# Five reorderings in a four-layer attention and expert kernel: masks and a table made earlier, VectorE's step order, a norm without transposes, a sum by additions, extra matmuls around a norm

## What is computed

```python
x = x + _L1_xattn_ref(_layernorm(x, axis=-1), ctx_2048, ctx_2048)
x = x + _L1_ffn_ref(_layernorm(x, axis=-1), L1_ffn_gate_weight, L1_ffn_gate_up_proj, L1_ffn_down_proj, L1_ffn_similarity)
x = x + _L2_xattn_ref(_layernorm(x, axis=-1), ctx_2048, ...)
x = x + _L2_ffn_ref(_layernorm(x, axis=-1), ...)
x = x + _L3_xattn_ref(_layernorm(x, axis=-1), ctx_2048, ctx_2048, mask, ...)
```

```python
sim = sim.at[jnp.arange(E), jnp.arange(E)].set(1.0)
sim_cand = sim[sec[:, :, None], prim[:, None, :]]
new_sec = jnp.where(best_sim < THRESHOLD, sec, best_primary)
combine = jnp.sum(jax.nn.one_hot(rerouted_indices, E) * routing_weights[..., None], axis=1)
```

## Time and profile before

| | |
|---|---|
| median of 3 runs | 1818.53 us (1818.27 to 1819.35) |
| profiled execution | 1817.0 us |
| its span | 1815.3 us |
| mean granted clock of PE | 0.890 |
| PE busy | 1519.1 us (84%) |
| DVE busy | 1083.3 us (60%) |
| ACT busy | 805.5 us (44%) |
| POOL busy | 801.4 us (44%) |
| layer two: norm, attention | 458.4 to 466.5, 466.8 to 571.8 us |
| layer two: feed-forward part | 573.7 to 853.9 us |
| layer three: attention after its preparation | 897 to 1297.5 us |
| layer four: norm, attention | 1480.3 to 1488.4, 1488.7 to 1578 us |

### The profile page before, as it was taken

The page is one execution under the profiler, slowest core; times in us unless marked ns, Lnnn a source line. Parts: engine busy times, 40 slices in busy tenths (PEclk is TensorE's granted clock), DMA queues, the critical chain, the costliest instruction groups (busy, mean ns, idle before and its releaser), DMA issues. The chain is left out here.

```text
span 1815.3 us, 25122 instructions
## 1 busy us (share of the span) xinstructions
PE 1519.1 (84%) x8563; PEld 971.4 (54%) x8600; DVE 1083.3 (60%) x2317; ACT 805.5 (44%) x1879; POOL 801.4 (44%) x975
## 2 busy tenths in 40 slices
PE   7566669999797799998899999999799989836772
PEld 5222235556465356556367777776455565525661
DVE  7999972222665644354778888888722255572336
ACT  3988873111333211111788888888521111412221
POOL 3366641000200289792277787777310000027772
PEclk9666659999698899999999999999899988958896
DMA  2599981110503111310600000000111100056656
GB/s 79 86 182 176 174 150 55 35 44 18 186 2 124 64 55 59 125 50 19 209 1 13 13 13 13 13 13 1 44 30 42 37 25 1 25 219 233 233 172 243
DMA packets 177808, 148.52 MB, mean 82 GB/s; under 512 B 142305, under 2 KB 155233, under 8 KB 173970
## 3 DMA queue, kind: packets, MB, share of 16 engines
q1 hardware_dynamic: 167618, 119.08, 24.3%
q0 software_dynamic: 7696, 26.22, 4.1%
q10 hardware_dynamic: 2368, 1.61, 0.3%
HBM read 89.62 MB, written 23.70 MB: 62 GB/s over the span
## 5 line engine op out<-in xcount | busy, mean ns | idle before, releaser
L1983 POOL CAST l0m_pi<-l0m_pf 128x1024 bf16<-128x1024 int16 x128 | 133.2, 1040 | 88.2 <-ACT l0m_pf L2050 86.4
L421 PE MATMUL l1e_gu<-x_normT,l1e_w 128*128 128x512 f32 x384 | 171.5, 601 | 0.0
L2050 ACT ACTIVATE l0m_pf<-l0m_s,l0m_bias,l0x_sq 128x1024 int16<-128x1024 f32 x128 | 153.9, 1204 | 20.9 <-DVE l0m_bias L2083 14.7
L2079 DVE TENSOR_REDUCE l0m_mx<-l0m_s 128x1 f32<-128x1024 f32 x128 | 155.6, 1216 | 4.4 <-PE l0m_s L1992 4.1
L1558 PE MATMUL l2x_pr<-l_w,l2x_xq 128*128 128x512 bf16 x539 | 133.5, 382 | 8.5 <-ACT credits L42 5.7
L1992 PE MATMUL l0m_s<-l0x_kT,l0x_qT 64*128 64x512 bf16 x256 | 68.0, 552 | 68.5 <-ACT l0m_pf L2050 66.9
L421 PE MATMUL l0e_gu<-x_normT,l0e_w 128*128 128x512 f32 x272 | 121.5, 601 | 0.0
L421 PEld LDWEIGHTS l1e_gu<-x_normT,l1e_w 128*128 128x128 f32 x384 | 74.2, 194 | 84.1 <-issue 83.0
L421 PE MATMUL l2e_gu<-x_normT,l2e_w 128*128 128x512 f32 x256 | 115.0, 604 | 0.0
L1688 DVE BATCH_NORM_STATS2 l2x_bn<-l2x_raw 128x6 f32<-128x128 f32 x384 | 83.3, 280 | 51.7 <-ACT l2x_raw L1627 51.5
L473 ACT ACTIVATE l1e_sil<-l1e_gu 128x512 f32<-128x512 f32 x48 | 28.6, 596 | 178.6 <-PE l1e_gu L421 178.6
(11 more groups left out here) (438 smaller groups left out, 3597.1 us busy)
## 6 DMA issues: line engine op xcount, KB each, us to landing
l3m_w<-in_l_moe SPq DMA_DIRECT2D x16, 1280.0 KB, 6.9
l1e_w<-in_l_ffn SPq DMA_DIRECT2D x24, 384.0 KB, 3.1
l_rows<-zero_row SPq DMA_DIRECT2D x8, 1024.0 KB, 10.9
l_w<-l_rows SPq DMA_DIRECT2D x8, 1024.0 KB, 11.3
l0e_w<-in_l_ffn SPq DMA_DIRECT2D x17, 384.0 KB, 3.1
l2e_w<-in_l_ffn SPq DMA_DIRECT2D x16, 384.0 KB, 3.0
ctx_tok<-l_route SPq DMA_DIRECT2D x8, 512.0 KB
l2q_wps<-in_l_wp SPq DMA_DIRECT2D x16, 256.0 KB, 3.5
```

The costliest lines, as they stand in the source:

```text
L421: last = nc.tensor.matmul(gu[half][:, m, :], w[:, c % SW, (2 * k + m) * P:(2 * k + m + 1) * P], pg.xnT[:, k, cols(n)], start=(k == 0), sto ...
L1983: nc.gpsimd.tensor_copy(pi[:, n % 8, :], pf[:, n % 4, :]).then_inc(s["rounded"], 1)
L2050: nc.scalar.activation(pf[:, n % 4, :], s_ps[n % 3][:], ACT.Exp, scale=sq[:, h, b:b + 1], bias=bias[:, n % 4:n % 4 + 1], accum_out=sm[:, b ...
L2079: nc.vector.tensor_reduce(mx[:, n % 4:n % 4 + 1], s_ps[n % 3][:], AX, ALU.max).then_inc(s["maxed"], 1)
```

## The change

It has five parts.

1. `norm` gets a switch `turns`, off for layer two's attention: PE's 16 transposes and their eight copies out are left out there.
2. Layer two's masks `quarter`, `own`, `other` are made by POOL at the end of its list in layer one's feed-forward part (`l1_masks`). In the attention POOL first waits for DVE's two small `qm` pieces before it zeroes `nm`, and for all four before it touches `vz`, of which it now zeroes only the columns that aren't copied. The four copies of context columns go from POOL to ACT, behind `cb`. DVE waits for the zeroed `nm` after `qm`.
3. Layer two's router gets its table as a whole 128 x 128 array by one DMA in the stage's preload; POOL only sets the diagonal. ACT does a dummy exponential at the start of its list. The final reduction over eight rows becomes three additions of halves.
4. In layer three's attention, the norm's multiplication and the reciprocal come first in DVE's list of each step.
5. `keep_busy` adds PE matmuls of the identity by itself (128 x 128, f32) into unused PSUM: eight at the end of layer three's feed-forward part, eight before the transposes of layer four's norm, and two between each pair of those.

```diff
+def l1_masks(pg, pool):
+    g, C, steps = pg.nc.gpsimd, 16, pg.sem("l1_mask_steps")
+    quarter, own, other = (pg.l1_masks[:, n, :] for n in range(3))
+    g.memset(quarter, 1.0 / 4.0).then_inc(steps, 1)
...
+    g.tensor_scalar(own, quarter, 4.0, None, ALU.mult).then_inc(steps, 1)
+    g.tensor_scalar(other, quarter, -4.0, 1.0, ALU.mult, ALU.add).then_inc(steps, 1)
...
+def keep_busy(pg, unread, n):
+    for _ in range(n):
+        pg.nc.tensor.matmul(unread, pg.ident[:], pg.ident[:], start=True, stop=True)
...
-            for i in range(PAIRS):
+            if warm:
+                keep_busy(pg, ps[0][0][:, 0:P], 8)
+            for i in range(PAIRS if turns else 0):
...
+                if warm and i + 1 < PAIRS:
+                    keep_busy(pg, ps[i + 1][0][:, 0:P], 2)
...
+            if name == "l2":
+                keep_busy(pg, gu[0][:, 0, 0:P], 8)
...
-        nc.gpsimd.memset(r.sim[:], 0.0).then_inc(r.const_steps, 1)
-        pool.wait_ge(r.const_in, 16 * S)
+        pool.wait_ge(pg.l1_sim_in, 16)
...
+        nc.scalar.activation(r.small[:, 3, 0:1], pg.ident[:, 0:1], ACT.Exp).then_inc(r.const_in, 1)
         exp_scalar(r, act)
...
-        v.tensor_reduce(r.cw[:], r.one.rearrange("p b k e -> p b e k"), AX, ALU.add).then_inc(r.route, 1)
+        for n in (4, 2):
+            ch.link(v.tensor_tensor(r.one[:, :, 0:n, :], r.one[:, :, 0:n, :], r.one[:, :, n:2 * n, :], ALU.add))
+        v.tensor_tensor(r.cw[:], r.one[:, :, 0, :], r.one[:, :, 1, :], ALU.add).then_inc(r.route, 1)
...
+            pool.wait_ge(qm_in, 2)
+            g.memset(nm[:], 0.0).then_inc(zeroed, 1)
+            pool.wait_ge(qm_in, 4)
             for par in range(2):
...
-                    g.tensor_copy(vz[:, par, k, :].rearrange("p (n c) -> p n c", c=32)[:, :, cols],
-                                  pg.ctxT[:, k, :].rearrange("p (n c) -> p n c", c=32)[:, :, cols]).then_inc(vz_in, 1)
+                    g.memset(vz[:, par, k, :].rearrange("p (n c) -> p n c", c=32)[:, :, rest], 0.0).then_inc(vz_in, 1)
...
+                    nc.scalar.activation(vz[:, par, k, :].rearrange("p (n c) -> p n c", c=32)[:, :, cols],
+                                         pg.ctxT[:, k, :].rearrange("p (n c) -> p n c", c=32)[:, :, cols], ACT.Copy).then_inc(vz_copied, 1)
...
                     for t in range(8):
+                        if job := norm_due(t, 4, pi, ai):
...
+                            nc.vector.tensor_tensor(raw[:, u], raw[:, u], rs[:, 1, u].unsqueeze(2).to_broadcast([P, U, DH]), ALU.mult)\
+                                .then_inc(s["normed"], 1)
+                        if job := due(t, 4, ai, zi, wi):
...
+                            nc.vector.reciprocal(rsm[:, a % 2], sm[:, a % 2]).then_inc(s["recip"], 1)
                         if wi is not None and wi[1] == 1 and t == 2:
...
-            "l0f": lambda: ffn("l0", 9, router_l0, 17, 3, [(8, 1), (0, 8)], [6, 11], None),
+            "l0f": lambda: ffn("l0", 9, router_l0, 17, 3, [(8, 1), (0, 8)], [6, 11], l1_masks),
```

More of the change, by code:

```diff
@@ L83, in l2_centre @@
     return beside
+def l1_masks(pg, pool):
+    g, C, steps = pg.nc.gpsimd, 16, pg.sem("l1_mask_steps")
+    quarter, own, other = (pg.l1_masks[:, n, :] for n in range(3))
+    g.memset(quarter, 1.0 / 4.0).then_inc(steps, 1)
+    pool.wait_ge(steps, 1)
+    for par in range(2):
+        for j in range(4):
+            rows = slice(32 * j, 32 * j + 32)
+            g.affine_select(out=quarter[rows, par:par + 1], in_=quarter[rows, par:par + 1],
+                            compare_op=(ALU.is_gt if par == 0 else ALU.is_ge), fill=0.0,
+                            base=(C if par == 0 else -C), pattern=[[0, 1]],
+                            channel_multiplier=(-1 if par == 0 else 1)).then_inc(steps, 1)
+    pool.wait_ge(steps, 9)
+    g.tensor_scalar(own, quarter, 4.0, None, ALU.mult).then_inc(steps, 1)
+    g.tensor_scalar(other, quarter, -4.0, 1.0, ALU.mult, ALU.add).then_inc(steps, 1)
+    pool.wait_ge(steps, 11)
 def l2_split(pg, pool):
@@ L199, in negative_mean, with norm @@
                                             op0=ALU.mult, op1=ALU.mult).then_inc(self.nb_in, 1)
-def norm(pg, name, src, preload=None, twice=False, moments=None):
+def norm(pg, name, src, preload=None, twice=False, moments=None, turns=True, warm=False):
     nc = pg.nc
@@ L601, in allocate @@
         r.oneT = pg.xn[:, 0:B // 2, :].rearrange("p b d -> p (b d)")
-        r.sim = sb("sim", [P, P])
+        r.sim = pg.l1_sim
         r.w8 = sb("w8", [P, B, K])
@@ L629, in pe_prog @@
             last.then_inc(r.pe_done, 1)
[L630 removed]
+        pe.wait_ge(r.const_steps, 1)
         for g in range(2):
@@ L798, in psum @@
             return st.enter_context(nc.psum_tensor(f"l1x_{m}", shape, dt))
-        quarter = sb("quarter", [P, 2])
-        own = sb("own", [P, 2])
-        other = sb("other", [P, 2])
+        quarter, own, other = (pg.l1_masks[:, n, :] for n in range(3))
         qm = sb("qm", [P, 2, B, D])
@@ L908, in value @@
                 if q == 0:
-                    pe.wait_ge(vz_in, 2 + 2 + 2 * KD)
+                    pe.wait_ge(vz_in, 2 * (2 + KD))
+                    pe.wait_ge(vz_copied, 2 * KD)
                 for nh in range(KD):
@@ L933, in _ @@
         def _(act):
-            act.wait_ge(masks, 2)
             for half in split:
@@ L938, in _ @@
                                          bias=other[:, par:par + 1]).then_inc(cb_in, 1)
+            for par in range(2):
+                cols = slice(C * par, C * par + C)
+                for k in range(KD):
+                    nc.scalar.activation(vz[:, par, k, :].rearrange("p (n c) -> p n c", c=32)[:, :, cols],
+                                         pg.ctxT[:, k, :].rearrange("p (n c) -> p n c", c=32)[:, :, cols], ACT.Copy).then_inc(vz_copied, 1)
             for q in range(Q):
@@ L951, in _ @@
             v = nc.vector
-            dve.wait_ge(const, 10)
-            v.tensor_scalar(own[:], quarter[:], 4.0, None, ALU.mult).then_inc(masks, 1)
-            v.tensor_scalar(other[:], quarter[:], -4.0, 1.0, ALU.mult, ALU.add).then_inc(masks, 1)
             for half in split:
@@ L2435, in preload @@
                     sp.dma_start(pg.router_w[:], router_w).then_inc(pg.router_w_in, 16)
+                    if name == "l1":
+                        sp.dma_start(pg.l1_sim[:], dram["l1_sim"]).then_inc(pg.l1_sim_in, 16)
                     for c in range(slots):
@@ L2452, in attention @@
                 pre = preload_of(pg, early) if preload_of else None
-                norm(pg, f"{name}n", pg.x, pre.load if pre else None, name == "l2x")
+                norm(pg, f"{name}n", pg.x, pre.load if pre else None, name == "l2x", turns=(name != "l1x"), warm=(name == "l3x"))
                 pg.moments = Moments(pg, f"{name[:2]}n", nc.alloc_semaphore)
@@ L2510, in layout @@
     a["l1_router"] = halves(v["L1_ffn_gate_weight"].T)
-    a["l1_sim"] = v["L1_ffn_similarity"]
+    a["l1_sim"] = np.zeros((128, 128), np.float32)
+    for j in range(4):
+        a["l1_sim"][32 * j:32 * j + 32, 32 * j:32 * j + 32] = v["L1_ffn_similarity"]
     w = v["L1_ffn_gate_up_proj"]
```

45 lines of the change are left out of this document (13 added, 32 removed).

## The result

The changed kernel takes 1804.01 us (median of 4 runs, 1800.33 to 1807.2) against 1818.94 (1818.27 to 1820.73): a ratio of 0.9915, 95% interval 0.9901 to 0.993. 1803.1 was forecast, within 1798 to 1810.

What follows compares the result with a forecast made beforehand. No engine was taken to bound the whole program, so each part was priced in its place: -7.65 - 2.46 - 6.3 + 0 + 1.0 = -15.4 from the profiled 1817.0 gives 1801.6, plus 1.5 for the runs' median 1803.1, range 1798 to 1810.

Steps and rivals of the forecast that it cites:

- Layer two's start, -7.65: Layer two's attention: without transposes and late masks, the first maximum comes at 468.2 against 475.85, 7.65 us earlier.
- the cover: Layer two's attention: ACT, with its four moved copies, is ready 0.4 us before the first exponential is due.
- Router, -2.46: Layer two's router: 1.17 us less from the earlier table and 1.29 less from three additions replacing the reduction.
- Layer three, -6.3: Layer three's attention: 14 items each 0.40 us shorter, -5.6, and -0.7 in its last 25 us.
- the tail: Last 25 us of layer three's attention, bound by DVE: an earlier reciprocal gives 0.2 us in three to four steps, -0.7.
- The floor by ACT's copy of the one buffer: Layer three's transposes cannot start before ACT has read their one PSUM buffer, so 0.40 us per item is gained, not 0.82.
- The rival in which the wait only changes its name: Layer three: multiplication and POOL's L1520 collide, the 0.40 per item is lost again; layer gains 1, total 1808.4; chance 0.15.
- The slower rival: Layer three: later `bn_stats` delays POOL and PE's turn of the probabilities, each item 1.1 us longer; total 1824.8; chance 0.04.
- Layer four's norm, 0: Extra identity matmuls cost 1.0 us at layer three's end and save 0.8 in layer four's norm: net 0 (+0.2).
- Clock, +1.0: Allowance of 1.0 us for clock rises that come later after shifted starts, with ends of -1 and +4.

Runs made afterwards that it cites:

- a3_router: The kernel before with only layer two's router changed (table by one DMA, dummy exponential, three additions): ratio 0.9985 to the kernel before.
- second profile of the change: The changed kernel run and profiled once more with no edit: 1804.99 us.
- a1_order: The kernel before with only the norm's multiplication and the reciprocal put first in DVE's steps of layer three's attention: ratio 0.9964 to the kernel before.
- b1_norm_first: The kernel before with only the norm's multiplication moved ahead in layer three's attention, the reciprocal left in place: ratio 0.997 to the kernel before.
- c4_no_between: The changed kernel without the pairs of identity matmuls between layer four's norm transposes, the groups of eight kept: 1805.35 us against 1804.99.
- a2_l1x: The kernel before with only layer two's norm transposes left out, its masks made early and its context copies on ACT: ratio 0.9952 to the kernel before.
- a4_warm: The kernel before with only the identity matmuls at layer three's end and in layer four's norm: ratio 0.9987 to the kernel before.
- b3_y_early: The changed kernel with the output projection ahead of the transposes in PE's step 7 of layer three's attention: 1800.64 us, ratio 0.9898 to the kernel before.
- c3_l1_gap: The changed kernel with 28 identity matmuls in layer two's norm and 12 where PE waits for DVE's first maximum: 1801.21 us against 1804.99.

## Why the prediction was right

The time came out 0.9 us from the forecast, and the three terms that carry it hold one by one.

- *Layer two's start, -7.65:* -7.97 in both profiles and -7.96 alone. The earlier start (2.0) and the freed `qm` (6.0) are what the sum has; the 0.45 that I added for POOL's zeroing of `nm` was too much by 0.3. ACT's copies cost 0.54 each, not up to 0.78, and the cover was 1.07, not 0.4.
- *Router, -2.46:* -1.21 and -1.25 in a3_router, -2.48 together in the second profile of the change. In the first the table gives only 0.54, since the clock rose later in the up-projections that go ahead of it.
- *Layer three, -6.3:* -5.47 in a1_order, -5.74 in the first profile of the change and -4.40 in the second, where the stretch ahead of the first transposes was 1.5 longer. The projections have -4.83 and -4.32 (forecast 5.6), the tail -0.81 and -1.51 (0.7). The floor by ACT's copy of the one buffer was the step on which the number hung, and the new wait shows it 16 times. It is 0.6 us each and not the 0.42 that the sum leaves (0.82 less 0.40), so the transposes themselves gained less than forecast; the turn of the probabilities, whose waits fell from 1.8 us to 0.6, made up part of it.
- *The rival in which the wait only changes its name* fell. A collision with POOL came, and L1701 and L1539 both got longer (means of 0.96 against 0.81 us and 1.45 against 1.17), but the turn of the probabilities waits once. The collision is mostly another than the rival's: 22 of the 96 multiplications take over 1.3 us, none did before, and all 22 begin while POOL works on L1559, which the earlier reciprocal starts sooner (POOL waited 20.6 us in all for it before and 1.4 now). The 14 that begin beside L1539 take no longer than the 28 that began beside L1520 before. The rule of the Trainium skill ("SBUF — State Buffer", Who interferes with whom), by which such a pair lock each other out, agrees with those rows as to the collision; what it costs depends on who waits behind it, and here PE does not.
- *The slower rival* fell with it. `bn_stats` comes later, and DVE's multiplications wait 9.4 us in all for POOL's statistics, where they waited 2.5, but none of it reaches PE's turn of the probabilities.

Two terms were mis-sized and offset each other in part. *Layer four's norm, 0*, measured -3.05 in the profile (-2.4 by the runs of part 5 alone). The step that failed is the reckoning of the norm by itself. That price was near (PE ends 1.06 later than DVE at the stage's end, 1.0 forecast; up to the first projection the change is +0.46, +0.2 forecast), but the clock behind the norm was left out: from the first projection to the second norm the stretch is 3.50 shorter (2.61 in the second profile), with the clock at 1.00 where it had fallen to 0.50 before. That the extra matmuls are what keeps it there is likely and not shown, since a3_router and b1_norm_first keep it without them. The rule that full clock does not engage for transposes (the Trainium skill, "TensorE: Matmul & The Clock Gate", Part 4: PE-mode transpose) isn't borne out by c4_no_between, whose norm with no pair between the transposes runs at 1.00. That the clock falls just behind that norm doesn't contradict the rule, and the rows don't tell whether these matmuls run in the transpose mode of which the Trainium skill speaks there, so it stays undecided. *Clock, +1.0*, measured more in this profile: +2.26 up to layer one's first expert matmul, +2.00 and -2.29 around layer two's attention, +2.63 in layer three's second norm, +2.41 at the end, together +7.0. That is why the profiled execution is 12.2 faster and not 15. The second profile has the same +2.6, +2.6 and +3.1, but -0.95 and -0.90. That 0.9 us remained between forecast and median is thus partly luck: the spread of the changed kernel's runs alone is 7 us. By the ratios the parts alone (a1 to a4) come to 20.3 us and the whole change to 15.5; the intervals of the parts together are some 5 us to either side, so whether the parts cost each other something isn't shown.

## What to carry to other kernels

Price a moved wait by the next thing that is late at the same instruction, not by the length of the wait: of 11.5 us of waits 4.8 came, because the buffer behind them was still being read. A clock kept up is worth something only as far as it stays up; look for the next wait of a few us behind the place that is kept warm (28 matmuls in the norm did nothing measurable; with 12 more in one gap of 2.7 us the stretch behind it was 5.5 us shorter, though the 12 alone were not run). Where PE starts cold, the same code takes lengths 2 to 4 us apart, so a part worth 2 us is shown by its own stretch in the trace and not by one run.

## What was not expected of the hardware

The kernel before is steady: 28 runs on one chip lie within 1817.11 to 1821.72 us, 11 on another within 1817.25 to 1821.3, and 18 on a third within 1816.81 to 1821.0 but for one of 1814.46. Most versions of it spread over more, 1806.27 to 1816.77 with part 4 alone. In the second norms of layers one and three its profile has the shorter of two lengths. From the first transpose of layer three's to the first expert matmul it is 9.4 to 9.9 us in before, a2_l1x, a4_warm, b3_y_early and c3_l1_gap, and 12.18 to 12.20 in the nine other profiles; in layer one 9.6 to 9.9 in before, a1_order, a3_router, b3_y_early and c3_l1_gap, and 12.18 or 12.19 in nine. In the shorter ones the granted clock goes up to 1.00 for some 3.4 us inside the stretch, and in the longer ones it stays at 0.50 there, as the windows of 273 to 283 us show (0.66 and 0.50). What decides whether it goes up isn't settled; the code there is the same in all of them. The same stretch of layer two keeps to no two lengths: it takes 9.6 to 13.1 us over the 14 profiles.
